# Full attention: 73 of 512 row maxima taken as difference, relu, add and maximum instead of one reduce

## The reference, cut to what matters

```python
q = (x @ Wq.T + bq).reshape(b, s, NHEADS, DK)      # b = 4, s = 1024, NHEADS = 16, DK = 8
k = (x @ Wk.T + bk).reshape(b, s, NHEADS, DK)
v = (x @ Wv.T + bv).reshape(b, s, NHEADS, DV)
w = jnp.einsum('bshd,bzhd->bhsz', q, k) / jnp.sqrt(jnp.float32(DV))
w = jax.nn.softmax(w, axis=-1)                     # over all 1024 keys z
vw = jnp.einsum('bhsz,bzhd->bshd', w, v).reshape(b, s, NHEADS * DV)
out = vw @ Wo.T + bo
```

## Time and profile before

| | us |
|---|---|
| median of three runs | 2025.06 (2024.56 to 2025.61) |
| the profiled execution's own time | 2022.25 |
| its span, first to last instruction | 2020.3 |
| full attention: first matmul to last copy | 949.8 to about 1629 |

### The profile page before, as it was taken

The page is one execution under the profiler, slowest core; times in us unless marked ns, Lnnn a source line. Parts: engine busy times, 40 slices in busy tenths (PEclk is TensorE's granted clock), DMA queues, the critical chain, the costliest instruction groups (busy, mean ns, idle before and its releaser), DMA issues. The chain is left out here.

```text
span 2020.3 us, 34429 instructions
## 1 busy us (share of the span) xinstructions
PE 1584.1 (78%) x11512; PEld 919.1 (45%) x11512; DVE 1352.2 (67%) x3452; ACT 1146.2 (57%) x2997; POOL 609.2 (30%) x680
## 2 busy tenths in 40 slices
PE   7799999999993399635999999999999954440870
PEld 3477877777773299522122222222222233340770
DVE  5655556656655142177999999999999656970643
ACT  3366666666662144343488888888888844210322
POOL 2133433633624765311001000100100011066574
PEclk8799999999996699866799999999999986655895
DMA  5155444411110477333000000000000000011754
GB/s 174 34 165 169 162 149 149 142 37 37 48 30 23 141 233 237 117 111 103 18 23 22 23 22 23 22 21 23 23 22 10 2 1 7 0 43 47 221 180 138
DMA packets 89787, 159.12 MB, mean 79 GB/s; under 512 B 18404, under 2 KB 56356, under 8 KB 89484
## 3 DMA queue, kind: packets, MB, share of 16 engines
q1 hardware_dynamic: 71884, 100.17, 16.8%
q0 software_dynamic: 17728, 56.76, 8.1%
HBM read 75.21 MB, written 65.54 MB: 70 GB/s over the span
## 5 line engine op out<-in xcount | busy, mean ns | idle before, releaser
L2137 DVE TENSOR_REDUCE q_max<-s_ps 128x1 f32<-128x1024 f32 x512 | 598.0, 1218 | 13.8 <-PE s_ps L2028 6.1
L2118 ACT ACTIVATE probs<-s_ps 128x512 f32<-128x512 f32 x1024 | 535.5, 602 | 124.3 <-PE s_ps L2049 124.2
L2028 PE MATMUL s_ps<-k_stack,q_stack 64*128 64x512 bf16 x1024 | 351.4, 396 | 16.9 <-PEq L101 8.6
L2049 PE MATMUL s_ps<-q_stack,k_stack 64*128 64x512 bf16 x1024 | 319.4, 384 | 20.3 <-ACT probs L2118 15.9
L2063 PE MATMUL o_ps<-probs,v_aug 128*32 128x512 f32 x2048 | 273.6, 606 | 0.7 <-ACT probs L2118 0.7
L2049 PEld LDWEIGHTS s_ps<-q_stack,k_stack 64*128 64x128 bf16 x1024 | 78.4, 94 | 334.5 <-ACT probs L2118 282.6
L1010 POOL TENSOR_TENSOR probs<-probs,p_rsum 128x512 f32<-128x512 f32 x128 | 133.1, 1040 | 312.6 <-DVE p_rsum L987 311.8
L889 ACT ACTIVATE probs<-s_biased,s_min 128x128 f32<-128x128 f32 (+1 forms) x512 | 197.8, 391 | 39.7 <-DVE s_min L981 38.3
L1663 POOL CAST neg_max_parts<-neg_max 16x128 bf16<-16x128 f32 x32 | 9.0, 281 | 474.5 <-DVE neg_max L2145 474.5
L753 PE MATMUL score_ps<-k_pad,q_bd 128*128 128x128 f32 x1024 | 146.6, 287 | 0.0
L981 DVE CUSTOM_DVE_ANT_0 s_biased<-score_ps,nbias 128x128 f32<-128x128 f32 (+1 forms) x512 | 115.8, 281 | 42.2 <-PE score_ps L753 41.0
(11 more groups left out here) (328 smaller groups left out, 2837.4 us busy)
## 6 DMA issues: line engine op xcount, KB each, us to landing
moe_rows<-empty_rows POOLq DMA_DIRECT2D x36, 1020.0 KB, 5.3
moe0b_wblock<-in_L_ffn_blocks SPq DMA_DIRECT2D x39, 578.0 KB, 4.0
moe1b_wblock<-in_L_ffn_blocks SPq DMA_DIRECT2D x39, 256.0 KB, 3.6
v_shift<-v_tiles SPq DMA_DIRECT2D x32, 256.0 KB, 3.5
v_shift<-v_tiles SPq DMA_DIRECT2D x32, 224.0 KB, 4.1
qk_parts_dram<-qk_parts SPq DMA_DIRECT2D x16, 384.0 KB, 2.5
q_stack<-qk_parts_dram SPq DMA_DIRECT2D x192, 32.0 KB
k_stack<-qk_parts_dram SPq DMA_DIRECT2D x192, 32.0 KB
```

Of the source, the lines that this page charges most:

```text
L2028: mm = nc.tensor.matmul(s1[u % 2][:, c * CH:(c + 1) * CH], qs[head_rows(m), quad % 4, j, qt * P:(qt + 1) * P], ks[head_rows(m), quad % 4, ...
L2049: nc.tensor.matmul(bank_of("exp", 4 * k + pos)[:], ks[head_rows(m), quad % 4, j, kt * P:(kt + 1) * P], qs[head_rows(m), quad % 4, j, half ...
L2118: nc.scalar.activation(pr[:, k % 2, HEADS[pos], :], bank_of("exp", n)[:], ACT.Exp).then_inc(sm["exp"], 1)
L2137: v.tensor_reduce(mx[:, h % 4, col:col + 1], s1[u % 2][:], AX.X, ALU.max).then_inc(sm["maxed"], 1)
```

## The change

For 73 of the 512 units (`by_difference`: even, and either among the first 24 or divisible by 8) the maximum is taken in another way, by max(a, b) = relu(a - b) + b for the two halves a and b of the keys:

- GpSimd writes a negated copy `kn` of the second half of each quad's keys (`negate_keys`), one quad ahead.
- TensorE multiplies chunk 0 as before but leaves the accumulation open, and adds a third matmul of 512 columns with `kn` (L2059 of the changed file), so that the first half of the PSUM tile holds the difference.
- ScalarE writes the relu of that half into the SBUF tile `s_lift` (`lift_over`, L2148): in the first 24 units by itself, and from then on ahead of the four exponentials of a step, in the steps with k % 4 = 0.
- VectorE, for these units, waits for the relu and takes one combined instruction over 512 columns (`tensor_tensor_reduce`: second half plus relu, and their maximum) with a read of its accumulator, instead of the reduce over 1024 columns.

The diff:

```diff
--- before.py
+++ after.py
@@ -1838,7 +1838,7 @@
 
 ATT_SEMS = ("loaded0", "loaded1", "loaded2", "loaded3", "m1_mm", "maxed", "m_turned", "m_neg", "m_split",
             "m_stored", "m_loaded",
-            "s2_mm", "exp", "v_aug", "pv_mm", "o_out", "o_turned", "o_done", "o_rsum")
+            "s2_mm", "exp", "over_set", "over_mm", "lifted", "v_aug", "pv_mm", "o_out", "o_turned", "o_done", "o_rsum")
 
 
 def full_attention_stage(nc, K, A, wo, M):
@@ -1900,6 +1900,8 @@
         nm = K.sb("neg_max", [2 * TPB, P], ctx=st)
         nr = K.sb("neg_max_rest", [2 * TPB, P], ctx=st)
         mp = K.sb("neg_max_parts", [2 * TPB, 2, 3, P], BF16, ctx=st)
+        kn = K.sb("k_negated", [P, 2, 2, CH], BF16, ctx=st)
+        lift = K.sb("s_lift", [P, 2, CH], ctx=st)
         ro = K.sb("o_rsum", [P, 2, CPT, 4], ctx=st)
         s1 = [K.ps(f"s1_ps{i}", [P, T], st) for i in range(2)]
         s2 = [K.ps(f"s2_ps{i}", [P, CH], st) for i in range(3)]
@@ -1911,6 +1913,16 @@
         HU = UNITS // 2
         AHEAD = HU + 8
         HEADS = (0, 2, 3, 1)
+
+        def by_difference(u):
+
+            return u % 2 == 0 and (u < AHEAD or u % 8 == 0)
+
+        differences = {u: n for n, u in enumerate(filter(by_difference, range(NQ * UNITS)))}
+
+        def last_difference(quad):
+
+            return max(n for u, n in differences.items() if u // UNITS == quad)
 
         def turned_view(bank):
 
@@ -1999,6 +2011,16 @@
                     split3(nc.gpsimd, pool, sm["m_split"], 4 * h, nm[:], [mp[:, h % 2, j, :] for j in range(3)],
                            nr[:])
 
+                def negate_keys(quad):
+
+                    pool.wait_ge(sm[f"loaded{quad % 4}"], LOADS * (quad // 4 + 1))
+                    if quad >= 2:
+                        pool.wait_ge(sm["over_mm"], last_difference(quad - 2) + 1)
+                    nc.gpsimd.tensor_scalar(kn[:, quad % 2], ks[:, quad % 4, :, CH:T], -1.0, None, ALU.mult
+                                            ).then_inc(sm["over_set"], 1)
+
+                negate_keys(0)
+                negate_keys(1)
                 wo.gate(pool)
                 for quad in range(NQ):
                     if quad >= 2:
@@ -2013,6 +2035,8 @@
                         wo.add_bias(b)
                     if quad >= 1:
                         split_max(2 * quad - 1)
+                    if 1 <= quad < NQ - 1:
+                        negate_keys(quad + 1)
                     split_max(2 * quad)
                 split_max(2 * NQ - 1)
 
@@ -2025,9 +2049,15 @@
                         pe.wait_ge(sm[f"loaded{quad % 4}"], LOADS * (quad // 4 + 1))
                     if u >= 2 and c == 0:
                         pe.wait_ge(sm["maxed"], u - 1)
-                    mm = nc.tensor.matmul(s1[u % 2][:, c * CH:(c + 1) * CH],
-                                          qs[head_rows(m), quad % 4, j, qt * P:(qt + 1) * P],
-                                          ks[head_rows(m), quad % 4, j, c * CH:(c + 1) * CH], start=True, stop=True)
+                    q = qs[head_rows(m), quad % 4, j, qt * P:(qt + 1) * P]
+                    over = u in differences and c == 0
+                    if over:
+                        pe.wait_ge(sm["over_set"], quad + 1)
+                    mm = nc.tensor.matmul(s1[u % 2][:, c * CH:(c + 1) * CH], q,
+                                          ks[head_rows(m), quad % 4, j, c * CH:(c + 1) * CH], start=True, stop=not over)
+                    if over:
+                        nc.tensor.matmul(s1[u % 2][:, 0:CH], q, kn[head_rows(m), quad % 2, j, :],
+                                         start=False, stop=True).then_inc(sm["over_mm"], 1)
                     if c == 1:
                         mm.then_inc(sm["m1_mm"], 1)
 
@@ -2109,7 +2139,22 @@
                         act.wait_ge(sm["o_turned"], m - 1)
                     nc.scalar.copy(osb[:, m % 2, :], op[:]).then_inc(sm["o_out"], 1)
 
+                def lift_over(u):
+
+                    n = differences[u]
+                    act.wait_ge(sm["over_mm"], n + 1)
+                    if n >= 2:
+                        act.wait_ge(sm["maxed"], by_count[n - 2] + 1)
+                    nc.scalar.activation(lift[:, n % 2, :], s1[u % 2][:, 0:CH], ACT.Relu).then_inc(sm["lifted"], 1)
+
+                by_count = list(differences)
+                for u in range(AHEAD):
+                    if u in differences:
+                        lift_over(u)
                 for k in range(NK):
+                    for u in step_units(k):
+                        if u in differences:
+                            lift_over(u)
                     for pos in range(4):
                         n = 4 * k + pos
                         act.wait_ge(sm["s2_mm"], n + 1)
@@ -2134,8 +2179,14 @@
 
                         dve.wait_ge(sm["m_turned"], h - 3)
                     dve.wait_ge(sm["m1_mm"], u + 1)
-                    v.tensor_reduce(mx[:, h % 4, col:col + 1], s1[u % 2][:], AX.X, ALU.max
-                                    ).then_inc(sm["maxed"], 1)
+                    if u in differences:
+                        n = differences[u]
+                        dve.wait_ge(sm["lifted"], n + 1)
+                        r = v.tensor_tensor_reduce(lift[:, n % 2, :], s1[u % 2][:, CH:T], lift[:, n % 2, :], 1.0, -3e38,
+                                                   ALU.add, ALU.max, mx[:, h % 4, col:col + 1])
+                    else:
+                        r = v.tensor_reduce(mx[:, h % 4, col:col + 1], s1[u % 2][:], AX.X, ALU.max)
+                    r.then_inc(sm["maxed"], 1)
 
                 def negate_max(h):
 
```

## The result

The changed kernel takes 2045.59 us (median of four runs, 2043.63 to 2047.30), the kernel before 2024.81 beside it: a ratio of 1.0104, 95% interval 1.0092 to 1.0116, 20.8 us slower. The forecast was 2046, with 2033 to 2061 as its range.

The account below looks back on a forecast made before the run. A TensorE-ScalarE loop nearly level with VectorE was taken as the bound. Terms 10.8 + 6 + 1.1 + 1.4 + 1.5 = 20.8 us on the profiled 2022.25 gave 2043, forecast as a median of 2046, range 2033 to 2061.

Parts of the forecast that it names:

- Level loops: Full attention: the TensorE-ScalarE loop, 2.40 us per step, stands nearly level with VectorE's 2.32, so relieving VectorE gives little.
- Rival 1: Full attention: VectorE sets the pace and relus vanish in ScalarE's idle 15%; about 34 us faster, 1991; chance 0.09.
- Copy's step: Steps k % 8 = 0, with the output copy: the relu adds 0.36 us to ScalarE's full queue, 10.8 us in all.
- The other step: Steps k % 8 = 4: VectorE waits 0.85 us for the relu and ends late; 0.2 us a period, 6 us.
- Third matmul hidden: Steps with a relu: TensorE's extra 0.22 us slot is covered by the wait for VectorE and costs nothing.
- Rival 3: Steps with a relu: every relu costs its full slot and the third matmul its own; 2072 us; chance 0.11.
- First 24 units: Start of the stage at half clock: a pair takes 2.44 us through three engines; twelve pairs add 1.1 us.
- the bound with a faster clock: Start of the stage: if extra matmuls raise TensorE's clock to full, a pair takes 2.01 us, giving -4.1 us.
- Wait for the negation: Start of the stage: unit 0 waits for GpSimd's negation of 1024 bf16 columns; 1.4 us, bounds 0.9 to 2.4.
- later negations: After the start: they run in GpSimd's idle time and cost nothing unless one holds up a split of the maxima.
- Table load: Start of the stage: the 1.28 us load lands before the first exponential; 1.5 us net, bounds 0 and 4.9.
- Rival 2: Full attention: the relus cost and give nothing, the period stays 20.2, only the start remains; 2029 us; chance 0.06.

Follow-up runs that it names:

- e7: Kernel before, but units from 24 on with u % 8 = 0 get VectorE's combined instruction against a constant, without negation, third matmul or relu: 2023.7 us, period 20.22.
- e8: Kernel before, but all even units from 24 on get VectorE's combined instruction against a constant, without third matmul or relu: 2024.0 us, period 20.14.
- e3: Kernel before plus the change's difference from unit 24 on only where u % 16 = 8, the step with the output copy: 2038.0 us, period 20.57.
- e5b: The change from unit 24 on only (u % 8 = 0), with VectorE's combined instruction taking zeros and not waiting for the relu: 2037.3 us, period 20.62.
- e6: Kernel before plus negation and third matmul from unit 24 on (u % 8 = 0), without relu or combined instruction: 2022.1 us, period 20.22.
- e10: Kernel before plus the change's difference only where u % 16 = 12 (steps k % 8 = 2): ratio 1.0031, period 20.36.
- e9: Kernel before with the copy of the finished output moved from ScalarE to VectorE: 2020.07 us against 2023.67, ratio 0.9979, period 20.05.

## Why the prediction was right, point by point

- *Level loops, so relief for VectorE gives little:* shown by e7 (0.00) and e8 (0.08 of 20.22 for 4.3 us of relief). Rival 1 (1991 us) is out.
- *Copy's step, 0.36 us x 30 = 10.8:* e3 has 0.35, 29 periods, 10.2. The step itself grew by 0.28 and not 0.36 (0.50 + 0.47 + 1.44 + 0.46 = 2.87 for exponential, relu, three exponentials and copy, where I had six slots of 0.49); the step behind it, which I left as it was, grew by 0.07. That the two together come to the price I had is luck.
- *The other step, 0.2 us x 30 = 6:* 0.15, 4.4. The wait for the relu was foreseen at 0.85 and is 1.00: from the relu's end to VectorE's start it is 0.17 (1206.07 - 1205.90), where I had 0.05 from an exponential to a matmul. My reason, that VectorE hands its tile back late, carries 0.10 of the 0.15: e5b, without the wait, has 0.05 more than e3, and that is left to ScalarE, which runs from the relu through seven exponentials without a pause.
- *Third matmul hidden:* e6, 0.00 in the steps of the change; ahead of the transposes, in e10, it is not hidden. Rival 3 (2072) needed it uncovered, and both relus at full price; they cost 0.35 and 0.15, not 0.49 each.
- *First 24 units, +1.1:* 2.2. A pair takes 2.56 us, not 2.44: the chain of three engines was right, its hand-overs too small (to VectorE again, 0.14 from the relu's end at 960.75 to 960.89). The clock stayed at 0.50, so the bound with a faster clock did not come into play.
- *Wait for the negation, 1.4, bounds 0.9 to 2.4:* 3.0, outside the bounds. This term failed. I worked it from a memset, a copy and a two-input instruction of float32, and took the slowest of these as upper end; the negation of 1024 bf16 columns takes 2770 ns. Of 1024 columns only the two-input instruction was shown, and I chose below it. The later negations cost nothing, as said: e6 has them all and the period of before.
- *Table load, 1.5:* 2.3 more at the first exponential, of which 0.7 is regained by the first reciprocal, 1.6 net.
- *Sum:* 6.9 at the start (forecast 4.0) and 14.4 in the periods (16.8): 21.3, against 20.8 foreseen and 20.8 between the medians. The total is closer than its parts: I had the start 2.9 too low and the periods 2.4 too high, and that these cancel is luck. Rival 2, with the start alone, was wrong by the whole 14.4.

## What to carry to other kernels

Where two engines hand tiles to each other in a loop, the busy share doesn't say which of them pays: a step without a pause does, and a slot on an engine that is 85% busy can be dearer than one on an engine at 96%. Work that is moved is paid at the place where it lands: a relu of 0.49 cost 0.35 in a step without a gap and 0.15 in a step that had one, 0.10 of it because the tile came late to the next engine. What comes along with it is paid at its own place: the third matmul cost nothing where a wait covered it, and its whole slot of 0.22 ahead of the transposes. Before relieving the busy engine, try the opposite move, as e9 did: it costs one experiment and here it was the only one that paid.

## What the runs showed of the hardware that I had not expected

GpSimd, over the whole span (line, operation, count | busy us, mean ns | idle before):

```profile
L2019 POOL TENSOR_SCALAR k_negated<-k_stack 128x1024 bf16<-128x1024 bf16 x16 | 44.3, 2770 | 138.4 <-DMA q_stack<-q_stack 117.6
```

A one-input multiplication of 1024 bf16 columns takes 2770 ns, more than the 2361 of a two-input instruction of as many float32 columns.

The combined instruction on 512 columns, one input in PSUM, takes 0.69 us, and the next one starts 0.62 behind its start; the accumulator read of 0.08 starts together with that next one and adds nothing to the 0.62.

Relu and exponential alternate in the loop with no table load between them (0.48 us from the relu's start to the exponential's); the one load of 1.28 us stands in front of the first exponential, which starts 0.02 behind its end.

A hand-over from ScalarE to VectorE took 0.14 to 0.17 us from end to start, one from ScalarE to TensorE 0.05.
